# A selective-scan block with mixture of experts on one core: step sizes in two-block operations, and the first two C products of a pair written straight into its sums

## The reference, cut to what matters

```python
dt = softplus(xb @ W_dt + b_dt)
def step(h, inp):
    A_bar = exp(dt_t[:, :, None] * A)
    h = A_bar * h + (dt_t * x_t)[:, :, None] * B_t[:, None, :]
    y_t = einsum('bdn,bn->bd', h, C_t)
y = (y + D_param * xb) * silu(z)
x = x + ga * (residual + y @ W_out)
...                                   # layer norm, router: 4 of 16 experts
x = x + gb * sum_e weight_e * down_e(silu(gate_e x) * up_e x)
```

## Time and profile before

| what | value |
|---|---|
| median of three runs | 2831.99 us |
| the profiled execution | 2825.79 us, of which its span is 2824.0 us |
| busy, TensorE (matmul) | 2374.4 us, 84% |
| busy, VectorE (DVE) | 2432.5 us, 86% |
| busy, ScalarE (ACT) | 1562.2 us, 55% |
| busy, GpSimd (POOL) | 2326.8 us, 82% |
| DMA | 592.62 MB, mean 210 GB/s |
| chain that ended last | PE 40%, DVE 24%, issue 12%, POOL 9%, DMA 7%, ACT 7% |

### The profile page before, as it was taken

How to read it: one execution, slowest core, us unless ns; L and a number is a source line. 1 busy time by engine, 2 the same in 40 slices (tenths; PEclk the granted TensorE clock), 3 DMA queues, 4 the chain that set the end, 5 groups by cost and what they waited for, 6 DMA issues and landing times.

```text
span 2824.0 us, 29162 instructions
## 1 busy us (share of the span) xinstructions
PE 2374.4 (84%) x9004; PEld 1667.0 (59%) x9004; DVE 2432.5 (86%) x2482; ACT 1562.2 (55%) x2945; POOL 2326.8 (82%) x1563
## 2 busy tenths in 40 slices
PE   3445798989979798998979899898989989898799
PEld 1222466666756666665656667566666756566578
DVE  2678898989989998999989899998989899899832
ACT  3555665566556556655665665566566556664311
POOL 1688888889898888999888889898889889887922
PEclk7677899999999999998999999998999999999999
DMA  4588898888888988888898888888888888897921
GB/s 111 159 213 221 219 230 225 208 225 221 224 221 225 230 210 227 225 221 220 225 234 216 221 219 222 224 223 233 222 224 214 225 220 219 233 235 204 226 69 49
DMA packets 345293, 592.62 MB, mean 210 GB/s; under 512 B 50464, under 2 KB 161056, under 8 KB 345136
## 3 DMA queue, kind: packets, MB, share of 16 engines
q1 hardware_dynamic: 281392, 381.01, 42.9%
q0 software_dynamic: 63744, 209.74, 39.2%
HBM read 379.25 MB, written 10.06 MB: 138 GB/s over the span
## 4 chain that ended last, share of the span: by engine, by line
PE 40%; DVE 24%; issue 12%; POOL 9%; DMA 7%; ACT 7%; SPq 1%; DVEq 0%; POOLq 0%; ACTq 0%
PE wbank L478 14%; DVE hbank L701 13%; PE mbank L490 6%; POOL unit L1161 4%; PE wbank L420 4%; PE wbank L506 4%; PE wbank L380 4%; PE wbank L368 3%; DVE unit L708 2%; PE wbank L503 2%; DMA gsum<-unit 2%; DMA w_all<-w_scratch 2%; DMA w_scratch<-rows_out 2%; ACT z L817 2%; DVE act L679 2%
## 5 line engine op out<-in xcount | busy, mean ns | idle before, releaser
L1161 POOL TENSOR_TENSOR unit<-dtx,b_bc 128x1024 f32<-128x1024 f32 x512 | 1351.1, 2654 | 12.0 <-DMA b_bc<-bc_scratch 11.5
L701 DVE TENSOR_TENSOR_SCAN hbank<-hbank,unit 128x1024 f32<-128x1024 f32 x512 | 1173.4, 2292 | 107.0 <-ACT hbank L991 93.3
L991 ACT ACTIVATE hbank<-dt,a_neg 128x512 f32<-128x512 f32 x1024 | 669.1, 681 | 331.4 <-DVE unit L708 328.7
L708 DVE TENSOR_TENSOR unit<-hbank,c_bc 128x1024 f32<-128x1024 f32 x512 | 623.7, 1218 | 27.3 <-DMA c_bc<-bc_scratch 1.3
L490 PE MATMUL mbank<-down_t,act 128*128 128x256 f32 x2048 | 519.1, 392 | 64.9 <-POOL act L1129 38.4
L478 PE MATMUL wbank<-h_t,gate_t 128*128 128x256 f32 x2048 | 499.7, 388 | 23.9 <-DVE act L679 12.5
L1129 POOL TENSOR_TENSOR act<-act,w_all 128x512 f32<-128x512 f32 x256 | 357.2, 1396 | 184.2 <-DVE act L679 160.4
L1184 POOL DMA_DIRECT2D gsum<-unit x384 | 389.8, 1015 | 137.5 <-DMA gsum<-unit 62.9
L478 PE MATMUL wbank<-h_t,up_t 128*128 128x256 f32 x2048 | 486.9, 381 | 16.4 <-DVE gz L588 14.1
L490 PEld LDWEIGHTS mbank<-down_t,act 128*128 128x128 f32 x2048 | 391.8, 195 | 166.6 <-issue 62.6
L478 PEld LDWEIGHTS wbank<-h_t,gate_t 128*128 128x128 f32 x2048 | 389.2, 193 | 128.3 <-DVE act L679 26.9
(11 more groups left out here) (122 smaller groups left out, 2339.7 us busy)
## 6 DMA issues: line engine op xcount, KB each, us to landing
gsum<-unit POOLq DMA_DIRECT2D x384, 512.0 KB, 7.5
b_bc<-bc_scratch SPq DMA_DIRECT2D x512, 256.0 KB, 6.1
c_bc<-bc_scratch SPq DMA_DIRECT2D x512, 256.0 KB, 5.3
w_all<-w_scratch SPq DMA_DIRECT2D x256, 256.0 KB, 4.5
ht<-in_L_attn_x_dram SPq DMA_DIRECT2D x16, 512.0 KB, 8.5
w_out<-in_L_attn_W_out_dram SPq DMA_DIRECT2D x16, 512.0 KB, 10.0
ht<-in_L_attn_x_dram POOLq DMA_DIRECT2D x16, 512.0 KB, 6.4
out_dram<-xt SPq DMA_DIRECT2D x16, 512.0 KB, 3.3
```

Source lines behind the costliest of these rows:

```text
L701: eng.tensor_tensor_scan(h, h, unit[:, g % RING, :, :].rearrange("p a t -> p (a t)"), 0.0, ALU.mult, ALU.add).then_inc(scanned, 1)
L708: eng.tensor_tensor(unit[:, g % RING, :, :], hbank[g % HB][:, :, :], c_bc[:, s:s + 1, :].to_broadcast([P, 2, T]), ALU.mult).then_inc(c_sca ...
L991: eng.activation(hbank[g % HB][:, a, :], dt[:, 2 * q + a, :], ACT.Exp, scale=a_neg[:, 2 * q + a, n:n + 1]).then_inc(decayed, 1)
L1161: eng.tensor_tensor(unit[:, g % RING, :, :], dtx[:, 2 * q:2 * q + 2, :], b_bc[:, s:s + 1, :].to_broadcast([P, 2, T]), ALU.mult).then_inc(d ...
```

## The change

The exp and ln of the step sizes are taken once for both blocks of a pair (128 x 1024), in SBUF: relu goes to `dt` and abs to `dtx` (which is free until it is made), the bank is freed by the abs, exp and ln run in `dtx`, and GpSimd adds `dtx` to `dt` before it makes dtx. VectorE's four adds of a row are gone. The C products of units 0 and 1 are written by `times_c` into the two places of `gsum` itself, so GpSimd's two adds of a pair are gone and units 2 and 3 are added by DMA like the rest: 14 accumulating DMAs of a pair, not 12. The moments of several streams change. The core of the diff follows; of the two `step_sizes` in it that start with a loop the first is VectorE's and the second ScalarE's, and the three lines with `soft_p` stand in GpSimd's.

```diff
-    SUMS, LATER = 4, NS // 2 - 2
+    SUMS, LATER = 4, NS // 2 - 1
...
-    LAST_EXPERTS_AT = (33, 134)
+    LAST_EXPERTS_AT = (39, 138)
...
         def unit_freed(need, g):
             p, u = divmod(g, NS)
-            if u < 4:
-                need.wait_ge(added, 2 * p + u // 2 + 1)
+            if u < 2:
+                need.wait_ge(scanned, g + 1)
             else:
-                need.wait_ge(summed[u % 2], 16 * (LATER * p + (u - 4) // 2 + 1))
+                need.wait_ge(summed[u % 2], 16 * (LATER * p + (u - 2) // 2 + 1))
...
-                plan += [("mix1", behind, 4, 11, 14), ("load_gb", behind, 1, 54, 56),
-                         ("project", behind, 4, 15, 24), ("stats", behind, 5, 20, 26),
-                         ("turn", behind, 4, 27, 30), ("pick", behind, 5, 30, 32), ("weigh", behind, 2, 36, 37)]
-            plan += [("step_sizes1", slot, 9, 1, 7), ("load_wo", slot, 1, 24, 30), ("load_ga", slot, 1, 23, 26), ("scale_wo", slot, 1, 47, 47),
-                     ("scale_h", slot, 2, 56, 58), ("gates", slot, 9, 36, 42),
+                plan += [("mix1", behind, 4, 12, 15), ("load_gb", behind, 1, 65, 68),
+                         ("project", behind, 4, 15, 24), ("stats", behind, 5, 21, 26),
+                         ("turn", behind, 4, 29, 30), ("pick", behind, 5, 30, 32), ("weigh", behind, 2, 35, 37)]
+            plan += [("step_sizes1", slot, 9, 1, 16), ("load_wo", slot, 1, 41, 41), ("load_ga", slot, 1, 23, 28), ("scale_wo", slot, 1, 50, 50),
+                     ("scale_h", slot, 2, 57, 57), ("gates", slot, 9, 36, 42),
...
-                plan += [("load_x", coming, 1, 24, 29), ("norms", coming, 12, 31, 45), ("turn_in", coming, 2, 48, 55),
+                plan += [("load_x", coming, 1, 26, 30), ("norms", coming, 12, 31, 45), ("turn_in", coming, 2, 48, 55),
...
-                         ("rows_bc", coming, 3, 81, 83),
-                         ("step_sizes0", coming, 9, 73, 79)]
+                         ("rows_bc", coming, 3, 77, 80),
+                         ("step_sizes0", coming, 9, 74, 78)]
...
-            plan = [("mix1", last, 4, 5, 5), ("project", last, 4, 6, 6),
-                    ("stats", last, 5, 6, 8), ("turn", last, 4, 16, 18), ("load_gb", last, 1, 21, 26),
-                    ("pick", last, 5, 16, 16), ("weigh", last, 2, 24, 25)]
+            plan = [("mix1", last, 4, 9, 9), ("project", last, 4, 9, 9),
+                    ("stats", last, 5, 9, 11), ("turn", last, 4, 17, 18), ("load_gb", last, 1, 22, 26),
+                    ("pick", last, 5, 18, 18), ("weigh", last, 2, 23, 25)]
...
-            def step_sizes(row, q):
-                for m_ in (2 * q, 2 * q + 1):
-                    t = work.at["dt", row, m_]
-                    yield
-                    need.wait_ge(soft_act, 4 * (DK * row + m_ + 1))
-                    eng.tensor_tensor(dt[:, m_, :], dt[:, m_, :], t.bank[:, :], ALU.add).then_inc(t.free, 1)
...
             def times_c(g):
...
+                p, u = divmod(g, NS)
+                o = unit[:, g % RING, :, :] if u >= 2 else gsum[:, (2 * p + u) % SUMS, :, :]
+                if u < 2 and p >= 2:
+                    row, pair = divmod(p - 2, 2)
+                    y = work.at["y", row, 2 * pair + 1]
+                    need.wait_ge(y.full, y.after)
...
             def step_sizes(row, q):
                 for m_ in (2 * q, 2 * q + 1):
...
+                    else:
+                        need.wait_ge(driven, NU * (row - 1) + NS * (q + 1))
+                    eng.activation(dt[:, m_, :], t.bank[:, :], ACT.Relu, bias=b_dt[:, m_:m_ + 1])
+                    eng.activation(dtx[:, m_, :], t.bank[:, :], ACT.Abs, bias=b_dt[:, m_:m_ + 1]).then_inc(t.free, 1)
+                    yield
+                    yield
+                    yield
+                rest = dtx[:, 2 * q:2 * q + 2, :]
+                need.wait_ge(t.free, t.after)
+                eng.activation(rest, rest, ACT.Exp, scale=-1.0).then_inc(soft_act, 1)
+                need.wait_ge(soft_act, 2 * (2 * row + q) + 1)
+                eng.activation(rest, rest, ACT.Ln, bias=1.0).then_inc(soft_act, 1)
...
+                need.wait_ge(soft_act, 2 * n)
+                eng.tensor_tensor(dt[:, pair, :], dt[:, pair, :], dtx[:, pair, :], ALU.add).then_inc(soft_p, 1)
+                need.wait_ge(soft_p, n)
...
             def add(g):
                 p, u = divmod(g, NS)
-                if u in (0, 2):
+                if u < 2:
                     return
                 need.wait_ge(c_scaled, g + 1)
...
+                k = u % 2
+                if u >= 4:
+                    need.wait_ge(summed[k], 16 * (LATER * p + (u - 4) // 2 + 1))
+                eng.dma_start(gsum[:, (2 * p + k) % SUMS, :, :], unit[:, g % RING, :, :], accum_op=ALU.add).then_inc(
+                    summed[k], 16)
```

More of the change, by code:

```diff
@@ L231, in build @@
         rnorm_a, rnorm_p, rnormed = sem("rnorm_a"), sem("rnorm_p"), sem("rnormed")
-        driven, decayed, scanned, c_scaled, added = (
-            sem(n) for n in ("driven", "decayed", "scanned", "c_scaled", "added"))
+        driven, decayed, scanned, c_scaled = (sem(n) for n in ("driven", "decayed", "scanned", "c_scaled"))
         summed = [sem(f"summed{k}") for k in range(2)]
@@ L768, in _ @@
                         "silu_last": lambda r: silu_inputs(r, 1), "gates": gates,
-                        "step_sizes0": lambda r: step_sizes(r, 0), "step_sizes1": lambda r: step_sizes(r, 1),
                         "mix0": lambda r: mix(r, 0), "mix1": lambda r: mix(r, 1),
@@ L878, in step_sizes @@
                 for m_ in (2 * q, 2 * q + 1):
-                    t, at = work.at["dt", row, m_], 4 * (DK * row + m_)
+                    t = work.at["dt", row, m_]
                     need.wait_ge(t.full, t.after)
@@ L882, in step_sizes @@
                         need.wait_ge(mod_out, 16)
-                    x = t.bank[:, :]
-                    eng.activation(dt[:, m_, :], x, ACT.Relu, bias=b_dt[:, m_:m_ + 1]).then_inc(soft_act, 1)
-                    eng.activation(x, x, ACT.Abs, bias=b_dt[:, m_:m_ + 1]).then_inc(soft_act, 1)
-                    need.wait_ge(soft_act, at + 2)
-                    eng.activation(x, x, ACT.Exp, scale=-1.0).then_inc(soft_act, 1)
-                    need.wait_ge(soft_act, at + 3)
-                    eng.activation(x, x, ACT.Ln, bias=1.0).then_inc(soft_act, 1)
+                    else:
+                        need.wait_ge(driven, NU * (row - 1) + NS * (q + 1))
+                    eng.activation(dt[:, m_, :], t.bank[:, :], ACT.Relu, bias=b_dt[:, m_:m_ + 1])
+                    eng.activation(dtx[:, m_, :], t.bank[:, :], ACT.Abs, bias=b_dt[:, m_:m_ + 1]).then_inc(t.free, 1)
                     yield
@@ L1099, in step_sizes @@
                     yield
-                for m_ in (2 * q, 2 * q + 1):
-                    t = work.at["dt", row, m_]
-                    need.wait_ge(t.free, t.after)
+                n = 2 * row + q + 1
+                need.wait_ge(soft_act, 2 * n)
+                eng.tensor_tensor(dt[:, pair, :], dt[:, pair, :], dtx[:, pair, :], ALU.add).then_inc(soft_p, 1)
+                need.wait_ge(soft_p, n)
                 xb_ready(need, row)
@@ L1166, in add @@
                 p, u = divmod(g, NS)
-                if u in (0, 2):
+                if u < 2:
                     return
                 need.wait_ge(c_scaled, g + 1)
-                k = u // 2 if u < 4 else u % 2
-                o = gsum[:, (2 * p + k) % SUMS, :, :]
-                if u < 4:
-                    if p >= 2:
-                        row, pair = divmod(p - 2, 2)
-                        y = work.at["y", row, 2 * pair + 1]
-                        need.wait_ge(y.full, y.after)
-                    eng.tensor_tensor(o, unit[:, (g - 1) % RING, :, :], unit[:, g % RING, :, :],
-                                      ALU.add).then_inc(added, 1)
-                else:
-                    if u < 6:
-                        need.wait_ge(added, 2 * p + 2)
-                    else:
-                        need.wait_ge(summed[k], 16 * (LATER * p + (u - 6) // 2 + 1))
-                    eng.dma_start(o, unit[:, g % RING, :, :], accum_op=ALU.add).then_inc(summed[k], 16)
+                k = u % 2
[3 more added lines that the diff above has]
+                    summed[k], 16)
             eng.memset(ident[:, :], 0.0).then_inc(consts, 1)
```

6 lines of the change are left out of this document (2 added, 4 removed).

## The result

The changed kernel took 2855.2 us in the median of five runs (2849.64 to 2858.68), the kernel before beside it 2833.2 us (2826.95 to 2836.25): a ratio of 1.0082, interval 1.0066 to 1.0097. It is slower, by 22 to 23 us where the forecast had 10.4. The profiled execution took 2853.52 us, of which its span is 2851.8, 27.8 more than before. The traced execution of the kernel before (2825.79 us) lies 4.8 to 7.4 us under that kernel's medians beside the runs here, so the differences that are read from the traces tend to be larger than those of the medians, as 27.8 against 22 us here.

A forecast was written before the change was run, and what follows sets the result against it. Each slot was a ring of links bound in turn by TensorE, norm and router, GpSimd and loads, TensorE, ScalarE, VectorE. Terms 18.2 - 6.8 - 1 = +10.4 us on 2832.0 gave 2842.4 us, range 2785 to 2866.

The forecast's parts named there:

- E: ScalarE's link from the step sizes' second product to scan 27: merged exp and ln make scan 27 1.3 us later.
- VectorE's adds worth 0 in A: Two removed adds of a row lie beside TensorE's unbroken work at the slot's start, so removing them gains 0.
- A: TensorE's link from the slot's start to `project`, busy 48.5 of 49.5 us; no change in its length was forecast.
- The part on the stream moments: Priced moved streams: `stats` 0.85 us earlier, `turn` giving back 0.4, the loads and `scale_wo` 0.
- sign of being wrong: Slots of 158 to 160 us, TensorE with holes in A, or GpSimd's sum waits far over 63 us.
- B: Link through the row before's norm and router: 0.45 us shorter per slot, bounds 0 to 0.85.
- The ends: First row +1 us, slot 0 -2, tail 0; together -1 us.
- C and D: GpSimd's and the loads' work up to unit 16, then TensorE up to the step sizes; no change in length priced.
- VectorE's time: Rival: VectorE paces the slot's TensorE links after all, so its adds and waits come off: 2773 us, chance 0.12.
- no load was saved between ln and decay: Rival: no table load between ln and a decay or between exp and ln, giving 2807 us, chance 0.03.
- The DMAs: Rival: accumulating DMAs fall behind and GpSimd's waits for sums double, 2870 to 2890 us, chance 0.10.
- E gets shorter: Rival: exp and ln do not precede unit 27's decay 1, scan 27 2.7 us earlier: 2786, or 2805 to 2815; chance 0.20.

The follow-up runs named there:

- both parts and old moments: Changed kernel with merged exp and ln and C products in the sums, but every stream moment and the tail as in the kernel before: 2822.49 us, 0.9975.
- after: The changed kernel itself, with the whole change and all its new stream moments, against the kernel before: 2855.2 us, 1.0082.
- pair 1 back: Changed kernel with only `step_sizes1` returned to moments 1 to 7: 2849.76 us, 1.0059 of the kernel before.
- pair 1 and `mix1` back: Changed kernel with `step_sizes1` returned to moments 1 to 7 and `mix1` to 11 to 14: 2838.38 us, 1.0028 of the kernel before.
- the old moments of pair 0: `step_sizes0` at 73 to 79 and `rows_bc` at 81 to 83; with only these returned in the changed kernel: 2838.14 us, 1.0018 of the kernel before.
- the right piece of the new order: Changed kernel with all moments as before except `stats`, `turn` and `weigh`, which keep the new ones: 2815.32 us, 0.9945 of the kernel before.
- the C part alone: Kernel before with its own moments and step sizes, only the C products written into the sums, units 2 and 3 added by DMA: 2826.53 us, 0.9984.
- the product computed twice: Changed kernel with one expert's up product per row computed twice, just before the down product that waits: 2851.53 us, 1.0081 of the kernel before.

## Why the prediction was right, and where it was short

**Direction and E: right.** The term of 1.3 us of a slot measured 1.22, by the mechanism named: exp and ln of both blocks between the two decays of unit 27. The wait of scan 27 was forecast at 3.5 us and is 3.31. The activation of 128 x 1024 was taken at 1.02 us and is 1.05 and 1.06 in slot 6. The Trainium skill, ScalarE: Activation LUTs, section What ACT_TABLE_LOAD costs, gives 186 ns and 0.833 ns an element for an activation with immediate scale and bias; an estimate from it for 1024 elements is 1.04 us, and the trace agrees. The same section adds a drain of about 1380 ns to each load of 1283; here exp ends at 1202.74 and ln starts at 1204.05, so a switch costs 1.3 us in this place and not 2.66.

**VectorE's adds worth 0 in A: right, with the old moments.** With both parts and old moments VectorE gains 2.83 us by scan 3 and has given back all but 0.07 at scan 9, where TensorE's unbroken work ends. That was called the weakest step, and it held.

**A as a whole: the step that failed.** The part on the stream moments priced `stats`, `turn`, the loads and `scale_wo`, and had no term for `step_sizes1` from 7 to 16 or for `mix1` from 14 to 15, though both stand in the diff and both issue TensorE's work in the link that I had called without a hole; it took the products of A to come "in nearly the same order". Nor did it follow what a late scan 27 does to TensorE: the pause ahead of the slot grew from 1.62 to 3.98 us, and the clock fell behind it. Its sign of being wrong ("TensorE with holes in A") is the one that came. Measured, A is +1.52 us of a slot against 0, and over slots 1 to 15 it adds up to 20.1 us, more than E's 14.9. The row that would have told it is TensorE's order of gate, step-size product, up and down at the slot's start, read against GpSimd's weight, which before arrives without slack.

**B: right in size, lost in after.** -0.45 was forecast. B scatters, but its shortest slots repeat to a few hundredths: 19.01 us with the old moments of the norm (before, and both parts with all old moments), 18.56 with the new ones and `step_sizes1` at 1 to 7, which is the forecast to the hundredth, and 19.15 in after. The 0.6 us hang on `step_sizes1` too, and on a step that the prediction priced at nothing with its condition beside it: the add and product of pair 1 on GpSimd were to be through before the norm's mean, "and if that cover were gone each us would be one of B". With `step_sizes1` to moment 16 they start 30.4 to 31.6 us into the slot (L1104, in slot 6 at 1095.02), and the cover is gone. GpSimd of after, slot 6, then ScalarE, then GpSimd with pair 1 back:

```profile
1107.27 0.85 POOL L1060 TENSOR_SCALAR nmean<-sums 128x4 f32<-128x4 f32 x1
```

```profile
1108.24 0.51 ACT L808 ACTIVATE z<-xt,nmean 128x256 f32<-128x256 f32 x1 [0.38 <-POOL nmean L1060]
```

```profile
1107.91 0.23 POOL L1060 TENSOR_SCALAR nmean<-sums 128x4 f32<-128x4 f32 x1 [0.15 <-ACT xt L929]
```

With pair 1 back GpSimd waits for ScalarE, as before; in after ScalarE waits 0.36 to 0.39 us for GpSimd's mean in each of the twelve slots, which is most of the 0.6.

**The ends.** Slot 0 gave 4.5 us, not 2; the tail cost 3.4, not 0. The 4.5 can't be laid to VectorE's adds: with all old moments slot 0 gave 0.2, and the runs with pair 1 back and with pair 1 and `mix1` back, whose slot 0 is the same program, gave 3.6 and lost 0.8. The tail's cost was between -0.6 and 3.3 us in the other runs with the new order of the tail, so that order alone isn't its cause, and I can't name it.

**The sum.** Forecast 18.2 - 6.8 - 1 = 10.4. In the trace slots 1 to 15 give +29.2, slot 0 -4.5, start and tail +3.1: 27.8, of which A is the part not forecast (slots 1 to 15 by links: A +20.1, E +14.9, B -2.2, C and D -3.5). Slots 3 to 14 are 163.6 to 167.0 us long, not the 162.5 given as the sign. The 2855.2 us lie inside the range of 2785 to 2866, but that is in part luck: the range was that wide for E, the ends and the rivals, and none of it was meant for A.

**The rivals.** VectorE's time did not come through, and no load was saved between ln and decay. The DMAs do not fall behind. *E gets shorter* was described with the decay ahead of exp and ln, and that order did occur, with the old moments of pair 0: scan 27 came 2.1 us earlier over units 25 and 26 as forecast (2.7), but the two units behind it gave it back: scan 28 waits 0.99 us for a decay behind the same block, and scan 29 waits 1.09 us for GpSimd's drive. I had not followed it two units further.

## What to carry to other kernels

A step that an engine issues in a link without a hole has no free place: read the order of the work around its new place and who delivers the input of what now comes earlier. When a merged operation makes a long block on an engine, follow it past the first waiter to the next. Where a mean comes out between two expectations, list it slot by slot: here it was two kinds of slots, 1.2 us apart. Change the structure with the old order first; here both parts were worth 0.25%, the right piece of the new order another 0.3%, and the rest of it lost 1.4%.

## What the runs showed of the hardware

TensorE's granted clock fell to 0.50, its lower level of 1.2 GHz, behind every pause of 3.98 us in slots 3 to 14 of the kernel after and of the run with `step_sizes1` and `mix1` back, and the eight matrix products behind it took 3.4 to 3.75 us and not 1.97. Behind pauses of 2.84 to 2.88 us (all old moments) the same eight took 1.97 us in two slots and 2.49 to 3.54 in ten, and behind pauses of 2.25 us (the product computed twice) 1.96 or 1.97 in six and 2.98 to 3.59 in six. Behind pauses of 1.62 to 2.00 us (before) they took 1.96 or 1.97 each time, but once, with the C part alone, 3.09 behind 1.99. The two windows of the kernel after (us, then busy of each engine, granted clock, DMA share, GB/s):

```profile
1052.00:1054.00 2.00, 0.00 (x0) 0.00 (x0) 1.90 (x3) 0.23 (x1) 1.76 (x2) 1.00 1.08 270
...
1056.00:1058.00 2.00, 2.00 (x6) 1.53 (x5) 2.00 (x3) 0.00 (x0) 2.00 (x2) 0.50 0.80 156
```

The fall shows behind the pause, when work has begun again. What it costs depends on what follows: about 1.2 us of A with `step_sizes1` and `mix1` back, in the slots where it lasts, nothing with all old moments, where TensorE otherwise waits for GpSimd. 448 accumulating DMAs of 512 KB landed in 7.8 us in the kernel after and in 7.5 with the C part alone, as 384 did before; the DMA engines had room for them at a share of 0.95.
